# Six of eight tiles normalised, transposed and gated before cross attention ends

## What is computed

```python
x = x + _L1_xattn_ref(_layernorm(x), ctx_2048, Wq, bq, Wkv, bkv, Wp, bp)
h = _layernorm(x)                                  # next sublayer
logits = h @ gate_w.T                              # 16 experts
scores = jax.nn.sigmoid(logits)
_, topk_idx = jax.lax.top_k(scores + bias, 2)
sel = take_along_axis(scores, topk_idx)
gating = sel / sel.sum(-1)
x = x + shared(h) + sum_e combine[:, e] * expert_e(h)
```

## Time and profile before

| | us |
|---|---|
| three runs: median (lowest, highest) | 984.23 (982.48, 991.62) |
| the profiled execution, whole time | 986.36 |
| its span (first to last instruction) | 984.5 |
| mean granted TensorE clock | 0.889 of full speed |
| busy: PE, DVE, ACT, POOL | 775.3, 733.8, 557.0, 564.2 |

### The profile page before, as it was taken

How to read it: one execution, slowest core, us unless ns; L and a number is a source line. 1 busy time by engine, 2 the same in 40 slices (tenths; PEclk the granted TensorE clock), 3 DMA queues, 4 the chain that set the end, 5 groups by cost and what they waited for, 6 DMA issues and landing times. The chain is left out here.

```text
span 984.5 us, 14033 instructions
## 1 busy us (share of the span) xinstructions
PE 775.3 (79%) x4673; PEld 498.4 (51%) x4673; DVE 733.8 (75%) x1291; ACT 557.0 (57%) x1028; POOL 564.2 (57%) x440
## 2 busy tenths in 40 slices
PE   4999989847777877778779988767777777789991
PEld 2554754425656666666664366623333333356551
DVE  4766258189999999999962755789999999354564
ACT  2314113278778687687751454678888888214440
POOL 3115200198999999999941032257777776215642
PEclk9999999979999879889999989977777767779996
DMA  5002030000000000000006000979999999222224
GB/s 176 1 0 86 1 107 29 0 1 1 0 1 1 1 1 1 0 1 1 1 1 220 11 1 1 285 143 184 187 174 172 171 162 184 61 73 75 81 72 160
DMA packets 149525, 69.61 MB, mean 71 GB/s; under 512 B 139003, under 2 KB 144909, under 8 KB 148302
## 3 DMA queue, kind: packets, MB, share of 16 engines
q1 hardware_dynamic: 147150, 62.42, 29.0%
q0 software_dynamic: 2304, 6.29, 2.2%
HBM read 27.46 MB, written 7.68 MB: 36 GB/s over the span
## 5 line engine op out<-in xcount | busy, mean ns | idle before, releaser
L750 POOL TENSOR_TENSOR r_pairs<-r_side_exp 128x945 f32<-128x945 f32 x128 | 225.4, 1805 | 0.0
L853 ACT ACTIVATE r_w<-r_w,r_scale 128x1001 f32<-128x1001 f32 (+1 forms) x128 | 144.9, 1135 | 72.4 <-DVE r_w L938 57.6
L1722 ACT ACTIVATE c_probs<-c_scores,c_bias,c_q_scale 128x1024 int16<-128x1024 f32 x128 | 154.2, 1204 | 30.5 <-DVE c_bias L1735 21.7
L804 PE MATMUL r_head_sum<-ident,r_w 128*128 128x128 f32 (+1 forms) x1024 | 136.2, 293 | 43.2 <-ACT ctxT L864 21.8
L1659 POOL CAST kv_parts<-c_probs 128x1024 bf16<-128x1024 int16 x128 | 132.4, 1041 | 54.8 <-ACT c_probs L1722 53.8
L1733 DVE TENSOR_REDUCE c_neg_max<-c_scores 128x1 f32<-128x1024 f32 x128 | 155.5, 1215 | 6.5 <-PE c_scores L1672 6.3
L804 PEld LDWEIGHTS r_head_sum<-ident,r_w 128*128 128x128 f32 (+1 forms) x1024 | 125.8, 154 | 61.6 <-issue 34.8
L1672 PE MATMUL c_scores<-c_kT,c_placed 128*128 128x512 bf16 x256 | 105.1, 505 | 51.6 <-ACT c_probs L1722 48.1
L930 DVE SCALAR_TENSOR_TENSOR r_chosen<-r_pairs,r_kept,r_z 128x1024 f32<-128x1024 f32 (+1 forms) x104 | 128.0, 1272 | 4.4 <-ACT r_pairs L843 2.5
L938 DVE TENSOR_TENSOR r_w<-r_pairs,r_chosen 128x1024 f32<-128x1024 f32 (+1 forms) x104 | 121.3, 1204 | 0.0
L780 PE MATMUL r_head_sum<-r_up,ctxT 128*128 128x256 f32 x224 | 62.7, 449 | 21.8 <-ACT ctxT L864 21.8
(11 more groups left out here) (332 smaller groups left out, 1494.1 us busy)
## 6 DMA issues: line engine op xcount, KB each, us to landing
en_w<-in_w SPq DMA_DIRECT2D x1, 2992.0 KB, 12.1
ew_w<-in_w SPq DMA_DIRECT2D x1, 2992.0 KB, 12.2
ew_w_near<-in_w_near SPq DMA_DIRECT2D x1, 2176.0 KB, 21.8
r_up<-in_up SPq DMA_DIRECT2D x1, 2048.0 KB, 9.9
c_pT<-kv_parts SPq DMA_TRANSPOSE x128, 3.3
token_rows<-e_xn SPq DMA_DIRECT2D x2, 1024.0 KB, 5.8
e_row<-pick_rows SPq DMA_DIRECT2D x8, 256.0 KB, 4.4
zero_rows<-b_zeros SPq DMA_DIRECT2D x1, 1360.0 KB, 14.9
```

The lines of the kernel that those rows point to most:

```text
L750: nc.gpsimd.tensor_tensor(pairs[:, v % MADE, BY_ACT * KEYS:].rearrange("p (a b) -> p a b", b=KEYS), a.broadcast_to([P, ROWS - BY_ACT, KEYS ...
L804: last = nc.tensor.matmul(head_sum[0:m, b // 4, (b % 4) * P:(b % 4 + 1) * P], w[:, v % RING, b * P:b * P + m], ident[:, :], start=(h == 0 ...
L853: nc.scalar.activation(w[:, v % RING, 0:COLS[f]], w[:, v % RING, 0:COLS[f]], ACT.Silu, scale=scale[:, t % 2, h:h + 1]).then_inc(silu_done, 1)
L1722: nc.scalar.activation(probs[:, u % RING, :], scores[:, u % SCORED, :, :].rearrange("p a b -> p (a b)"), ACT.Exp, bias=bias[:, t, h:h + 1] ...
```

## The change

- `norm_statistics` gets a parameter `first`: with 6 (SOON), epsilon is added for tiles 0 to 5 after tile 5 and for 6 and 7 after tile 7. `norm_pool` then does the power in two parts: the first on POOL after the cast of unit 117 (NORM_AT), the second at the stage's end.
- In `attend`, DVE normalises tiles 0 to 5 after adding tile 6, ahead of `normalise(7)`. PE transposes tiles 0, 1 after the mix of head 13 of tile 7, tiles 2, 3 after that of head 14, tile 4 between `finish_a(7)` and `finish_b(7)`, and tile 5 after `finish_b(7)`; then it computes the logits of the six tiles. ACT copies the six tiles and takes the sigmoid of their logits. The four identity products at the end are gone.
- `route` normalises, transposes, copies and gates two tiles. The identity products before the ranks are two instead of four; those after stay four.
- Gate and bias are loaded at the start of `attend`. The normalised rows lie in the memory of `ctxT` instead of in a buffer of their own, so DVE waits in `mix_experts` until both stores of the rows have landed. The scratch for one attention tile (`o`, `oT`) moves to xT's last 256 columns, and `neg_max` has two tiles instead of eight.

```diff
-def norm_statistics(nc, eng, sh, t):
+def norm_statistics(nc, eng, sh, t, first=NT):
     nc.vector.bn_stats(ln.stats[:, t, :], sh.x[:, t, :]).then_inc(ln.steps, 1)
-    if t >= 1:
+    if t >= 1 and t != first:
         nc.vector.bn_aggr(ln.mv[:, t - 1, :], ln.stats[:, t - 1, :]).then_inc(ln.steps, 1)
...
-    if t == NT - 1:
+    if t in (first - 1, NT - 1):
+        part = slice(0 if t == first - 1 else first, t + 1)
         nc.vector.bn_aggr(ln.mv[:, t, :], ln.stats[:, t, :]).then_inc(ln.steps, 1)
...
-        nc.vector.tensor_scalar(ln.rstd[:, :], ln.mv[:, :, 1], LN_EPS, None, ALU.add).then_inc(ln.var_ready, 1)
+        nc.vector.tensor_scalar(ln.rstd[:, part], ln.mv[:, part, 1], LN_EPS, None, ALU.add).then_inc(ln.var_ready, 1)
...
@@ attend, memory
-        o, oT = sh.xT[:, 0, 0:D], sh.xT[:, 1, 0:D].rearrange("p (c n) -> p c n", c=DC)
+        o, oT = xT[:, 0, N - D:], xT[:, 1, N - D:].rearrange("p (c n) -> p c n", c=DC)
+        ln.xn = g.xn
+        ln_turned, logits = scores[:, (UNITS_C - 3) % SCORED, :, :], scores[:, (UNITS_C - 2) % SCORED, 0, :]
+        NORM_AT = UNITS_C - HEADS_C + PLACE_AT + 1
@@ attend, SyncE
+            load_gate(sp, g, i)
             for u in range(UNITS_C):
@@ attend, GpSimd
                 nc.gpsimd.tensor_copy(rounded[:, u % ROUNDED, :], probs[:, u % RING, :]).then_inc(rounded_ready, 1)
-            norm_pool(nc, pool, sh.ln, sh.ln.norms + 1)
+                if u == NORM_AT:
+                    norm_pool(nc, pool, ln, ln.norms + 1, slice(0, SOON))
+            norm_pool(nc, pool, ln, ln.norms + 2, slice(SOON, NT))
@@ attend, TensorE
                     if h == PROJECT_AT and t >= 1:
                         finish_b(t - 1)
+                    if t == NT - 1 and h >= HEADS_C - 3:
+                        n = 2 * (h - (HEADS_C - 3))
+                        if n == 0:
+                            pe.wait_ge(exp_done, UNITS_C)
+                            pe.wait_ge(g.loaded, 32)
+                        if n < SOON - 2:
+                            norm_turn(nc, pe, ln, ident, ln_turned, tiles, n)
+                            norm_turn(nc, pe, ln, ident, ln_turned, tiles, n + 1)
             finish_a(NT - 1)
+            norm_turn(nc, pe, ln, ident, ln_turned, tiles, SOON - 2)
             finish_b(NT - 1)
-            keep_busy(nc, scores[:, 0, 0, :], ident, 4)
+            norm_turn(nc, pe, ln, ident, ln_turned, tiles, SOON - 1)
+            pe.wait_ge(ln.copied, tiles + SOON)
+            gate_logits(nc, g, xT, logits, range(SOON)).then_inc(g.logits_ready, 1)
@@ attend, ScalarE, after the units
+            for t in range(SOON):
+                norm_copy(nc, act, ln, xT[:, :, t * P:(t + 1) * P], ln_turned, tiles, t)
+            act.wait_ge(g.logits_ready, 1)
+            gate_scores(nc, g, logits, 0, SOON).then_inc(g.score_ready, 1)
@@ attend, VectorE
             residual(NT - 2)
+            dve.wait_ge(ln.rstd_ready, ln.norms + 2)
+            norm_rows(nc, ln, x, range(SOON))
             normalise(NT - 1)
@@ gate_buffers
+    g.xn = sh.ctxT[:, :, :].rearrange("p c n -> p (c n)").rearrange("p (t d) -> p t d", d=D)
@@ route, SyncE
-            sp.dma_start(gate[:, :, :], i["gate"]).then_inc(loaded, 16)
-            sp.dma_start(bias[:, :], i["bias"].broadcast_to([P, EXPERTS])).then_inc(loaded, 16)
             sp.wait_ge(ln.normed, ln.tiles + NT)
@@ route, TensorE
-            norm_tensor(nc, pe, ln, ident)
-            pe.wait_ge(loaded, 32)
+            for t in range(SOON, NT):
+                norm_turn(nc, pe, ln, ident, ln.turned, ln.tiles, t)
             pe.wait_ge(ln.copied, ln.tiles + NT)
...
-            last.then_inc(logits_ready, 1)
-            keep_busy(nc, ln.turned[:, 0, :], ident, 4)
+            gate_logits(nc, g, xT, logits[:, 0, :], range(SOON, NT)).then_inc(g.logits_ready, 1)
+            keep_busy(nc, ln.turned[:, 0, :], ident, 2)
@@ route, ScalarE
-            norm_scalar(nc, act, ln, lambda t: xT[:, :, t * P:(t + 1) * P])
-            act.wait_ge(logits_ready, 1)
...
+            for t in range(SOON, NT):
+                norm_copy(nc, act, ln, xT[:, :, t * P:(t + 1) * P], ln.turned, ln.tiles, t)
+            act.wait_ge(g.logits_ready, 2)
+            gate_scores(nc, g, logits[:, 0, :], SOON, NT).then_inc(g.score_ready, 1)
@@ route, VectorE
-            norm_vector(nc, dve, ln, x, chain)
+            dve.wait_ge(ln.rstd_ready, ln.norms + 2)
+            norm_rows(nc, ln, x, range(SOON, NT))
@@ mix_experts, VectorE
             dve.wait_ge(ew.loaded, EW_LOADS)
+            dve.wait_ge(s.rows_stored, 16 * KEPT)
```

More of the change, by code:

```diff
@@ L130, in norm_tensor, with norm_turn, norm_copy @@
     for t in range(NT):
-        pe.wait_ge(ln.normed, ln.tiles + t + 1)
-        if t >= 2:
-            pe.wait_ge(ln.copied, ln.tiles + t - 1)
-        for c in range(DC):
-            last = nc.tensor.transpose(ln.turned[:, t % 2, c * P:(c + 1) * P], ln.xn[:, t, c * P:(c + 1) * P], ident[:, :])
-        last.then_inc(ln.turned_ready, 1)
+        norm_turn(nc, pe, ln, ident, ln.turned, ln.tiles, t)
+def norm_turn(nc, pe, ln, ident, turned, tiles, t):
+    pe.wait_ge(ln.normed, tiles + t + 1)
+    if t >= 2:
+        pe.wait_ge(ln.copied, tiles + t - 1)
+    for c in range(DC):
+        last = nc.tensor.transpose(turned[:, t % 2, c * P:(c + 1) * P], ln.xn[:, t, c * P:(c + 1) * P], ident[:, :])
+    last.then_inc(ln.turned_ready, 1)
 def norm_scalar(nc, act, ln, place):
     for t in range(NT):
-        act.wait_ge(ln.turned_ready, ln.tiles + t + 1)
-        nc.scalar.copy(place(t), ln.turned[:, t % 2, 0:D].rearrange("p (c n) -> p c n", c=DC)).then_inc(ln.copied, 1)
+        norm_copy(nc, act, ln, place(t), ln.turned, ln.tiles, t)
+def norm_copy(nc, act, ln, to, turned, tiles, t):
+    act.wait_ge(ln.turned_ready, tiles + t + 1)
+    nc.scalar.copy(to, turned[:, t % 2, 0:D].rearrange("p (c n) -> p c n", c=DC)).then_inc(ln.copied, 1)
 def start_stage(nc, x, ident, identb, x_dram):
@@ L1339 @@
 HEADS_C = 16
+SOON = 6
 HD_C = D // HEADS_C
@@ L1830, in load_experts, with gate_buffers, load_gate, gate_logits @@
     sp.dma_start(ew.w2[1][FAR:, :, :], ew.zero_rows.rearrange("(p r) d -> p r d", r=RANKS)).then_inc(ew.loaded, 16)
+def gate_buffers(nc, ctx, sh):
+    sb, ps, sem = scope(nc, ctx, "g_")
+    g = sh.gate = Buffers()
+    g.xn = sh.ctxT[:, :, :].rearrange("p c n -> p (c n)").rearrange("p (t d) -> p t d", d=D)
+    g.w, g.bias = sb("w", [P, DC, EXPERTS]), sb("bias", [P, EXPERTS])
+    g.score = sb("score", [P, NT, EXPERTS])
+    g.loaded, g.logits_ready, g.score_ready = sem("loaded"), sem("logits_ready"), sem("score_ready")
+def load_gate(sp, g, i):
+    sp.dma_start(g.w[:, :, :], i["gate"]).then_inc(g.loaded, 16)
+    sp.dma_start(g.bias[:, :], i["bias"].broadcast_to([P, EXPERTS])).then_inc(g.loaded, 16)
+def gate_logits(nc, g, xT, bank, tiles):
+    for t in tiles:
+        for c in range(DC):
+            last = nc.tensor.matmul(bank[:, t * EXPERTS:(t + 1) * EXPERTS], xT[:, c, t * P:(t + 1) * P],
+                                    g.w[:, c, :], start=(c == 0), stop=(c == DC - 1))
+    return last
+def gate_scores(nc, g, bank, lo, hi):
+    return nc.scalar.activation(g.score[:, lo:hi, :].rearrange("p t e -> p (t e)"), bank[:, lo * EXPERTS:hi * EXPERTS], ACT.Sigmoid)
 def routed_experts(nc, sh, i, out_dram, out_stored):
@@ L1855, in route @@
         ln = norm_buffers(sb, ps, sh)
-        ln.xn = s.xn
-        gate, bias = sb("gate", [P, DC, EXPERTS]), sb("bias", [P, EXPERTS])
+        g = sh.gate
+        ln.xn = s.xn = g.xn
+        bias, score = g.bias, g.score
         number_i, lane_i, pick_i = sb("number_i", [P, SUB], I32), sb("lane_i", [P, 1], I32), sb("pick_i", [P, PICKS], I32)
@@ L1904, in _ @@
         def _(pe):
-            norm_tensor(nc, pe, ln, ident)
-            pe.wait_ge(loaded, 32)
+            for t in range(SOON, NT):
+                norm_turn(nc, pe, ln, ident, ln.turned, ln.tiles, t)
             pe.wait_ge(ln.copied, ln.tiles + NT)
-            for t in range(NT):
-                for c in range(DC):
-                    last = nc.tensor.matmul(logits[:, 0, t * EXPERTS:(t + 1) * EXPERTS], xT[:, c, t * P:(t + 1) * P],
-                                            gate[:, c, :], start=(c == 0), stop=(c == DC - 1))
-            last.then_inc(logits_ready, 1)
-            keep_busy(nc, ln.turned[:, 0, :], ident, 4)
+            gate_logits(nc, g, xT, logits[:, 0, :], range(SOON, NT)).then_inc(g.logits_ready, 1)
+            keep_busy(nc, ln.turned[:, 0, :], ident, 2)
             pe.wait_ge(consts, 9)
@@ L2295, in decoder @@
         expert_weights(nc, ctx, sh)
+        gate_buffers(nc, ctx, sh)
         cross_attention(nc, sh, i)
```

37 lines of the change are left out of this document (18 added, 19 removed).

## The result

The kernel before took 988.0 us in this comparison (median of 20 executions), the changed one 981.24 (20): ratio 0.9937, with an interval of 0.9916 to 0.9958, that is -6.2 us (-4.1 to -8.3). Forecast were -6.85, or 0.9930. Two later comparisons gave 0.9955 [0.9925, 0.9986] and 0.9936 [0.9912, 0.9959]; weighted by their intervals the three make 0.9940 [0.9926, 0.9954], -5.9 us. One execution of each kernel took 2921 and 2443 us; neither moves its median by more than 0.5. The two later comparisons ran on chips on which every version took 995 to 1005 us, so times are only compared within one comparison.

The account below looks back on a forecast made before the run. The 42 us seam between attention (DVE-bound) and experts (PE-bound) was taken to move everything behind it one for one: units +0.35, rest of attention's end +0.1, `route` -7.3, together -6.85; 984.23 - 6.85 = 977.4 us, range 973.0 to 981.5.

Parts of the forecast that it names:

- R2: Rival with chance 0.15, waits return at attention's end or in `route`: one gives about 979.1 us, two 980.8.
- Units, +0.35: Attention's units: one more aggregation (0.18) and addition (0.17) for tile 5 on DVE, in its bound stretch, +0.35 us.
- POOL's power at 0: Attention's units: POOL's power of 1.65 us between two casts is covered by POOL's slack, 0; 1.65 if not.
- Up to the last projection, 0: Attention's end: six normalisations (2.4 us) fit DVE's 4.34 us wait and PE's transposes are covered, 0; 1.4 us without cover.
- Rest of attention's end, +0.1: From last projection to next stage: tile 5 and six tiles' logits (5.2 us) replace the identity products, +0.1 us.
- `route`, -7.3: `route` with two tiles instead of eight and two fewer identity products before the ranks: 22.4 to 15.15 us, -7.3.
- `mix_experts`, 0: Start of `mix_experts`: DVE's added wait for the row stores costs 0, as they land long before 872.
- the forecast's own case: End of `route`: ranks at 1.2 GHz take 2.4 us, and PE's last identity products end 0.6 us after DVE.
- the wait comes back: Rival, chance 0.15: power delays last casts (1.65), transposes delay last tile (1.4), or last identity products run slow (1.8 us).
- The clock stays up at attention's end: Rival, chance 0.12: new transposes fill PE's gaps, projection and logits run at 2.4 GHz, 4.0 us less, 973.4.
- The experts run slow: Rival, chance 0.05: PE enters `mix_experts` at 1.2 GHz and stays there; 13 us of slow work would give 990.4.
- the tiles only move one for one: Rival, chance 0.02: six tiles cost at attention's end what `route` gives back, 0 of 6.85 gained, 984.2.

Follow-up runs that it names:

- None before the ranks: The changed kernel without the two identity products before the ranks: ratio 0.9962 [0.9935, 0.9989] to the kernel before.
- none after the ranks: The changed kernel without the four identity products behind the ranks: ratio 0.9966 [0.9937, 0.9994] to the kernel before.
- identity products only: The kernel before without the four identity products at attention's end and with two instead of four before the ranks, no tile moved: ratio 0.9991 [0.9957, 1.0025].

## Why the prediction was right, and where not

The sign and the size of the change held: -6.85 forecast, -6.2 measured at first, -5.9 in all, and the main route by which it came. Three terms failed. POOL's power, put at 0 in the units, came back through SyncE's queue as 0.5 us of late last mix (up to 1.0 in other profiles). The clock's rise in `route` was counted from the wrong operation, which made the forecast of `route` about 1 us too long. And the level and the noise were wrong: the forecast of 977.4 stood on a median of three runs, 984.23, where twenty gave 988.0, so that the changed kernel's 981.24 is 3.8 us above it; and -6.85 us was said to be too small to be told from no change, with 9.8 us as the limit, while the measured interval is +- 2.1 us and lies clear of no change. The range's upper end, 981.5, is also 0.7 above the sum from which it was taken (two of R2's waits, 980.8). By its own steps, in the profiled seam:

- *Units, +0.35.* The two operations stand where they were put; the addition for tiles 0 to 5 took 0.17 (825.89, L105, 128x6), as in the earlier trace rows. In the stretch itself, whose length moves by over 1 us from one profile to the next (190.7 to 192.0 before, 191.3 to 193.4 changed), 0.35 can't be seen.
- *POOL's power at 0.* This step failed. On POOL it went as forecast: 1.33 us for six tiles between two casts (831.21 to 832.54), the casts made up behind it, and 0.70 for the last two (857.01), beside PE's logits. What the forecast left out is the engine behind POOL. SyncE issues the transposes of the units back to back, 1.38 us apart, and could not make up the delay. No run moves the power by itself; this is read from the order of events and from the table, where the last scale follows lag and flight in every profile.
- *Up to the last projection, 0.* It was +0.49 in the first profile and +0.60 and +1.01 in the other two of the changed kernel; the lag is 0.4, 0.6 and 0.9 of that, the flight the rest. The forecast's own terms of this step held: the six normalisations fitted under DVE's wait (2.81 us of 4.34), and so did PE's transposes.
- *Rest of attention's end, +0.1.* Next stage +0.13. Logits 5.30 (5.2 forecast), at clock 0.50. Right; 24 loads at the 0.107 us of the Trainium skill (TensorE: Matmul & The Clock Gate, on LDWEIGHTS) would be an estimated 2.6, and the trace disagrees: 5.18 busy us of loads for 24 at 1.2 GHz.
- *`route`, -7.3.* It was -8.3. Up to the ranks each step came out within 0.2 (scores ready 4.17 after the start, ranks 7.83; forecast 4.35 and 7.95). The term that was mis-sized is the clock's rise. I counted 5.3 us from the start of the ranks; it came 5.7 after the start of the two identity products ahead of them, 1.7 after that of the ranks. So the ranks with their hand-over took 2.06 instead of 2.4, the last identity products all ran at 2.4 GHz, and they ended before DVE instead of 0.6 after it. "None before the ranks" shows the forecast's own case: `route` is 1.3 us longer.
- *`mix_experts`, 0.* The waits added there cost nothing that shows; clock 1.00, 105.6 us against 105.5. Right on the first chip, open within some 2 us on the others.

That the sum came so near is in part luck: a term that was 0.5 us too low and one that was 1.0 too high partly cancelled, and the execution from which the seam of before was read had a late rise of the clock. Against the mean of three profiles the seam gains 6.6 us and not 7.7.

Of the rivals, "the wait comes back" came in part, by the power (a lag of up to 0.97 us, of 1.65), and was outweighed by the clock. "The clock stays up at attention's end" did not come: in no profile of the changed kernel or its variants does the clock rise between 4 and 24 us after tile 6's addition. "The experts run slow" needs PE idle in front of them, as "none after the ranks" showed. That the tiles only move one for one is refuted by "identity products only" together with the changed kernel.

What the forecast had not seen is that the yardstick moves. I took one execution's rise of the clock as the kernel's, 5.3 us, and in the 13 profiles it comes 2.9 to 5.9 us after the first of the identity products that lead to it. For the kernel before, this moves the seam by 3 us; the changed one, which has no identity products at attention's end, stayed within 0.1 in three profiles, though its last scale and its `route` moved by 0.5 against each other.

## What to carry to other kernels

Work that an engine can do early pays twice where filler work stands in its place: the filler goes, and the queue behind it gets shorter, but take out only filler that delays something, and keep the piece that stands before the next dense stage. When you put an operation into an engine's slack, ask which engine takes that engine's results, and whether it could make up a delay: POOL could, SyncE behind it could not. And before you name the last condition of a late operation, look when each of its operands arrived; the one that stands right ahead of it on its own engine need not be it. And where a term hangs on the clock's rise, look at several executions before you write a constant for it.

## What the hardware showed that I had not expected

- The clock's rise after the same instructions is not fixed: 2.9 and 5.9 us after the first identity product at attention's end in two executions of one kernel, 3.2 and 5.7 for those before the ranks in two that differ in one wait far ahead.
- With PE idle from 866.8 to 871.5, the clock had fallen by 869.6, and four pairs of float32 products cost 1.51 and three times 1.38 us instead of 0.83 and 0.76, until it rose at about 876.5 ("none after the ranks"). Of the 2.4 us only 1.0 reached the path.
- A float32 product with 16 columns costs 0.22 us a record at 1.2 GHz (5.30 / 24) whatever stands around it; moving it saves nothing at the place, only in the order.
- One 16 KB packet of instructions lay in the flight of the last transpose in two runs, and in both the transpose landed 1.5 us late (4.6 us instead of 3.1). Over all profiles, transposes with such a packet in their flight took 4.3 to 4.6 us in the median, the others 3.3. The packet moves between variants, and even between executions of the changed kernel (5.6 to 8.1 us after tile 6's addition), so a loss of 1 us in a single profile needs this look before a cause is named.
- SyncE issued a transpose every 1.38 us and was busy 1.28 us with each. In the changed kernel's first profile a delay of its input by 0.9 us was still in its queue eight transposes later, where POOL had made up the same delay in three casts.
